# Two attention and expert layers on one core: the norm's small operations divided anew between GpSimd and VectorE, the output bias as a product of one row, and another order of the work

## The chip, the core and the metric

The kernel is one program on one core of a Trainium2 chip. Its engines are TensorE (PE; PEld is its weight load), VectorE (DVE), ScalarE (ACT), GpSimd (POOL) and SyncE (SP), which here only issues DMA transfers. The metric is the time of the whole program on the device in microseconds, lower is better; each version is run several times and the median counts.

## The reference, cut to what matters

Two transformer layers over x of 16 batches x 256 tokens x 128 channels, fp32, each with attention (16 heads of 8) and a mixture of experts, and a layer norm without scale or shift after every half:

```python
def _layernorm(x, axis=-1, eps=1e-05):
    m = jnp.mean(x, axis=axis, keepdims=True)
    v = jnp.var(x, axis=axis, keepdims=True)
    return (x - m) / jnp.sqrt(v + eps)
...
x = _layernorm(x + _L0_attn_ref(x, ...))   # causal, no bias
x = _layernorm(x + _L0_ffn_ref(x, ...))    # 8 experts, top 2, hidden 256, relu
x = _layernorm(x + _L1_attn_ref(x, ...))   # not causal; w_out, b_out
x = _layernorm(x + _L1_ffn_ref(x, ...))    # 15 experts, top 3, gated gelu, and a shared expert
```

The bias of the second attention's output, `out @ w_out.T + b_out`, is what the change calls the output bias (the value bias is folded into it: `bias_rows`, `bias_add`).

## The kernel before, in words

**Steps.** The program is a list of some 3,990 named steps, such as `qk(a)`, `scores(a, p)` or `gather(q, blk, k)`. `plan()` names each step's engine and predecessors; the table `BEGINS` gives each a time of beginning in hundredths of a microsecond, and `lay_out` sorts the steps by it. These times are keys of an order and nothing else. Every engine runs its own steps in that order and waits on semaphores inside each; a step that waits holds everything behind it on its engine, SyncE's and GpSimd's DMA issues too. Between the steps of TensorE stand `WARM` entries, bursts of 128x512 products of ones (L1537), 242 in all.

**Attention.** Batch a = 0 to 15 is the first layer, 16 to 31 the second. `qk` makes queries and keys; `qk_hi`, `qk_rest`, `qk_mid`, `qk_low` split them into three bf16 parts. `spread_parts(a)` (L994) sends them to memory and `stack(a)` (L1009, six transfers) brings them back as 48 rows for eight pairs of heads. `scores(a, p)` and `row_max(a, p)` (L1586) find each query's maximum, which `max_neg`, `max_T`, `max_keep` and `max_rows(a)` (L1016, two transfers) put beside the keys; then `scores_T(a, p)`, `exp(a, p)` (L1218), `weigh_V` (L1404), `O_T`, `O_norm`, `O_back`, `O_back_keep`, `proj` (L1430) and `sum` (L1619).

**Norm.** `stats(k, q)` on VectorE takes the statistics and their aggregate (L1632, L1635); `inverse_std(k, q)` on GpSimd adds epsilon (L1108), negates the mean (L1109), raises to -0.5 (L1111) and multiplies both (L1113); `normalise(k, q)` on ScalarE applies it (L1253). k = 0 is the norm after attention, k = 1 after the experts. The 16 last norms (k = 1, q from 16) differ: VectorE adds epsilon (L1638), GpSimd raises two batches at once (L1102), VectorE normalises (L1646).

**Experts.** `x_T2`, `logits`, `route_top`, `route_hot`, `ranks`, `route_rank`, `route_pos_mul`, `route_pos` place each token on pages of 256 rows; `route_diff`, `route_exp`, `route_weight` make its weight. `scatter` (L1149, GpSimd) writes tokens to the page buffer `xs`, which `clear_xs(k)` (L980, SyncE, 22 transfers of 512 KB) fills with zeros first. `table(i)` and `table_row(i)` (L1747, L1022) say which expert owns a page. `x_load`, `w_load` (L1038), `page_T`, `fc1` (L1486), `activate`, `fc2` (L1498), `page_keep`, `page_store` (L1056) work off 108 pages in three groups: batches 0 to 7, 8 to 15 and 16 to 31. `gather` (L1163, GpSimd) fetches a token's results and `combine` (L1791) adds them. `build_w1(k)` (L985 to L988, SyncE) copies the second layer's expert weights into one table in eight pieces of three transfers. `residual_bias(a)` (L1092) adds the output bias to x on GpSimd, once for each batch of the second layer.

Of the kernel before, what the change touches and what calls it, by code (L numbers as in the profile page):

```python
# [9 lines left out]
ALU = mybir.AluOpType  # L10
# [3 lines left out]
NB = 16  # L14
T = 256
D = 128
# [209 lines left out]
def plan():  # L226
# [10 lines left out]
    def norm(kind, q, t, after):  # L237
        last = kind == 1 and q >= NB
        add(t, "DVE", 0.8 if last else 0.71, 0.1, "stats", kind, q, after=after)
        if not last or power_batches(q):  # L240
            add(t + PRM["norm"][0], "POOL", 0.76 if last else 1.45, 0.1, "inverse_std", kind, q, after=[("stats", kind, q)])
        add(t + PRM["norm"][1], "DVE" if last else "ACT", 0.55 if last else 0.81, 0.1, "normalise", kind, q,
            after=[("inverse_std", kind, q + 1 if last and not power_batches(q) else q)])

    def attention(a, t):
# [10 lines left out]
        x = [("load_xT", a), ("load_consts",)] if L == 0 else [("x_T_keep", a), ("load_later",)]  # L256
# [35 lines left out]
        add(t + pj[2], "PE", 0.56, 0.25, "proj", a, after=[("O_back_keep", a), ("residual_bias", a)] + [("load_x", i) for i, (lo, hi) in enumerate(X_PIECES) if lo <= a < hi],  # L292
# [115 lines left out]
    for b in range(NB):  # L408
# [8 lines left out]
    "load_x": (3936, 5173, 7563, 10838,),  # L417
    "load_later": (5993,),
    "prepare": (7562,),
    "bias_rows": (10638,),  # L420
    "bias_add": (10690,),
    "build_w1": (9858, 10628, 12703, 15096, 16526, 17957, 19532, 21073,),
    "clear_xs": (5233, 5283, 5943, 6438, 7622, 7672, 10068, 10118, 10898, 10948, 12913, 12963, 15306, 15356, 16736, 16786, 18166, 18216, 19742,
        19792, 21556, 21606,),
    "load_xT": (0, 42, 1415, 2245, 3244, 6745, 8164, 9409, 10999, 13030, 14578, 16065, 17476, 19954, 21515, 25665,),
    "qk": (922, 2026, 3021, 4013, 5072, 7612, 8805, 9864, 12531, 14111, 15200, 16703, 18246, 20823, 22543, 26343, 28727, 30936, 32258, 33253, 36798,
        38253, 39534, 43076, 46491, 48104, 49075, 51012, 52231, 54201, 56839, 58521,),
    "qk_hi": (1140, 2244, 3243, 4135, 5194, 7734, 8927, 9982, 12649, 14233, 15333, 16825, 18368, 20945, 22665, 26461, 28850, 31054, 32376, 33371,
        36920, 38371, 39656, 43198, 46613, 48226, 49197, 51134, 52367, 54323, 56961, 58639,),
    "qk_rest": (1203, 2307, 3306, 4280, 5321, 8003, 8990, 10143, 12849, 14360, 15449, 17072, 18495, 21148, 22792, 26524, 28936, 31303, 32525, 33515,  # L430
        37337, 38553, 39845, 43285, 46755, 48386, 49357, 51276, 52521, 54593, 57200, 58815,),
    "qk_mid": (1276, 2380, 3379, 4353, 5394, 8076, 9072, 10217, 12954, 14433, 15522, 17145, 18568, 21267, 22905, 26642, 29027, 31506, 32678, 33606,
        37428, 38644, 39994, 43453, 46937, 48496, 49448, 51383, 52612, 54684, 57382, 58923,),
    "qk_low": (1342, 2446, 3454, 4427, 5485, 8223, 9138, 10290, 13078, 14575, 15617, 17240, 18659, 21375, 22971, 26708, 29102, 31674, 32744, 33793,
        37544, 38744, 40098, 43519, 47012, 48566, 49582, 51533, 53042, 54857, 57577, 59087,),
    "spread_parts": (1456, 2519, 3527, 4526, 5558, 8296, 9211, 10364, 13151, 14648, 15690, 17313, 18810, 21448, 23045, 26831, 29175, 31747, 32817,
# [1454 lines left out]
```

## Time and profile before

| | |
|---|---|
| median of 3 runs | 905.49 us (899.75 to 909.22) |
| profiled execution | 905.51 us, span of its instructions 903.7 us |
| busy: PE, DVE, ACT, POOL | 773.8, 652.9, 500.9, 426.0 us |
| granted TensorE clock, mean | 0.96 |
| DMA | 144.56 MB, mean 160 GB/s |
| chain of waits: PE, DVE, DMA, issue, POOL, ACT | 27, 11, 6, 6, 3, 3% of the span |

Busy time is a sum over the whole span, PE's with the warm-up products in it. The chain of waits follows back what released the last instruction. It names the engine that was late each time, not how much later the next one would have been. In a timeline row the bracket gives the engine's idle time before the instruction and who ended it.

### The profile page before, as it was taken

Reading aid. Unit: us, or ns where it says so; the run is one execution under the profiler, and the core shown is the slowest. Engines: PE = TensorE matmul, PEld = TensorE weight load, DVE = VectorE, ACT = ScalarE, POOL = GpSimd, SP = SyncE. Lnnn points to the kernel's source line nnn. Section 1 sums busy time; section 2 is a strip of 40 time slices with the busy share of each in tenths; the row PEclk is TensorE's granted clock in tenths of the full one; section 3 lists DMA queues with packets and bytes.
Section 4 is the critical chain, followed back from the end, with each engine's and each line's share of the span. In section 5 each row is a group of like instructions: output and inputs, shape, how many; then the busy total and the mean of one; then the engine's idle time right before and its main releaser. Section 6 shows DMA issues by size and latency. Waiting matters only on the chain.

```text
span 903.7 us, 23670 instructions
## 1 busy us (share of the span) xinstructions
PE 773.8 (86%) x7908; PEld 514.9 (57%) x7908; DVE 652.9 (72%) x1916; ACT 500.9 (55%) x971; POOL 426.0 (47%) x654
## 2 busy tenths in 40 slices
PE   3799999887999889998999999989888898999900
PEld 2456556545777555554775655544444587789800
DVE  1768777776666579898668899889884354688845
ACT  2157557444656557577666877776656344444300
POOL 4002341242203665576235673567567501677775
PEclk9999989999999999999999999999999999999955
DMA  5796774788777555637875664525241189996723
GB/s 121 131 260 137 191 208 125 202 200 209 197 185 187 126 119 120 154 87 190 212 202 146 174 139 96 112 51 124 55 120 42 48 249 291 329 290 181 213 64 111
DMA packets 118775, 144.56 MB, mean 160 GB/s; under 512 B 13155, under 2 KB 92673, under 8 KB 118657
## 3 DMA queue, kind: packets, MB, share of 16 engines
q1 hardware_dynamic: 108417, 122.06, 52.0%
q0 software_dynamic: 10240, 20.99, 8.7%
q8 instruction: 67, 1.10, 0.5%
q14 instruction: 51, 0.42, 0.2%
HBM read 89.78 MB, written 54.41 MB: 160 GB/s over the span
## 4 chain that ended last, share of the span: by engine, by line
PE 27%; DVE 11%; DMA 6%; issue 6%; POOL 3%; ACT 3%; SPq 0%; POOLq 0%; DVEq 0%; ACTq 0%
DMA G<-yd,ypos 4%; DVE mp L1586 4%; PE bank_N L1498 3%; PE bank_O L1404 3%; PE bank_FH L1486 3%; ACT P L1218 2%; PE pair_T L1385 2%; POOL xs L1149 2%; PE pair_S L1363 2%; PE pair_T L1486 2%; DVE X L1791 2%; PE bank_O L1486 1%; PE pair_S L1486 1%; PE pair_T L1498 1%; PE bank_M L1475 1%
## 5 line engine op out<-in xcount | busy, mean ns | idle before, releaser
L1586 DVE TENSOR_REDUCE mp<-pair_S 128x4 f32<-128x1024 f32 (+1 forms) x248 | 270.3, 1090 | 73.6 <-PE pair_S L1363 71.9
L1218 ACT ACTIVATE P<-pair_T 128x768 f32<-128x768 f32 (+1 forms) x256 | 234.4, 916 | 97.0 <-PE pair_T L1385 93.4
L1163 POOL DMA_INDIRECT G<-yd,ypos x160 | 154.0, 962 | 109.4 <-DMA yd<-yb 57.1
L1149 POOL DMA_INDIRECT xs<-X,ypos x160 | 159.0, 994 | 80.3 <-issue 44.1
L1404 PE MATMUL bank_O<-P,V 128*18 128x256 f32 (+1 forms) x2048 | 112.0, 360 | 1.4 <-ACT P L1218 1.4
L1385 PE MATMUL pair_T<-QK 51*128 51x256 bf16 (+1 forms) x1024 | 95.8, 262 | 11.0 <-ACT P L1218 8.9
L1363 PE MATMUL pair_S<-QK 48*128 48x256 bf16 (+1 forms) x992 | 92.9, 264 | 7.5 <-DVE mp L1586 5.9
L1108 POOL TENSOR_TENSOR rstd<-mv,half 128x2 f32<-128x2 f32 x48 | 9.5, 198 | 167.4 <-DVE mv L1635 167.2
L1404 PEld LDWEIGHTS bank_O<-P,V 128*18 128x18 f32 x2048 | 54.7, 99 | 43.9 <-issue 13.0
L1791 DVE SCALAR_TENSOR_TENSOR X<-G,wk,X 128x128 f32<-128x128 f32 x160 | 56.2, 352 | 31.6 <-DMA G<-yd,ypos 28.2
L1385 PEld LDWEIGHTS pair_T<-QK 51*128 51x128 bf16 x1024 | 47.0, 96 | 33.5 <-ACT P L1218 24.2
L1363 PEld LDWEIGHTS pair_S<-QK 48*128 48x128 bf16 x992 | 37.1, 96 | 40.4 <-DVE mp L1586 23.6
L1347 PE MATMUL pair_T<-bmat 64*128 64x128 bf16 (+1 forms) x544 | 47.7, 252 | 12.9 <-DMA QK<-mrow 7.3
L1498 PE MATMUL bank_N<-W,hT 128*128 128x128 f32 x368 | 52.7, 287 | 3.4 <-DVE X L1619 2.9
L1347 PE MATMUL pair_S<-bmat 64*128 64x256 bf16 x480 | 42.3, 254 | 15.3 <-DMA QK<-stk 9.6
L1537 PE MATMUL bank_M<-bmat 128*128 128x512 bf16 x193 | 54.6, 387 | 0.2 <-issue 0.2
L1225 ACT ACTIVATE OT<-bank_O 128x256 f32<-128x256 f32 x64 | 24.3, 380 | 51.3 <-PE bank_O L1404 51.1
L1486 PE MATMUL bank_FH<-xpT,W 128*128 128x256 f32 x184 | 50.8, 399 | 1.4 <-issue 1.2
L1498 PEld LDWEIGHTS bank_N<-W,hT 128*128 128x128 f32 x368 | 45.9, 194 | 10.8 <-issue 4.1
L1270 ACT ACTIVATE hT<-bank_FH,W 128x256 f32<-128x256 f32 x92 | 38.6, 471 | 20.5 <-PE bank_FH L1486 19.9
L1324 PE MATMUL bank_M<-xT,wqk 128*128 128x256 f32 x128 | 40.3, 441 | 7.3 <-DMA wqk<-wqk_in 4.2
L1253 ACT ACTIVATE X<-X,rstd 128x128 f32<-128x128 f32 x96 | 41.9, 487 | 6.6 <-POOL rstd L1113 6.2
(178 smaller groups left out, 1432.8 us busy)
## 6 DMA issues: line engine op xcount, KB each, us to landing
QK<-wtab SPq DMA_DIRECT2D x62, 257.0 KB, 3.8
W<-w_in SPq DMA_DIRECT2D x46, 321.0 KB, 3.9
yd<-yb SPq DMA_DIRECT2D x53, 256.0 KB
stk<-parts SPq DMA_DIRECT2D x32, 384.0 KB
QK<-stk SPq DMA_DIRECT2D x64, 192.0 KB
xs<-zeros SPq DMA_DIRECT2D x19, 512.0 KB, 7.4
xp<-xs SPq DMA_DIRECT2D x33, 256.0 KB, 5.2
QK<-stk SPq DMA_DIRECT2D x64, 128.0 KB
```

The lines of the kernel that those rows point to most:

```text
L1149: pool.indirect_dma_start(xs[g % 2][0:reach(a) * PAGE], bass.IndirectOffsetOnAxis(ypos[L][:, 2 * b + blk, k:k + 1], 0), X[:, 2 * b + blk, ...
L1163: pool.indirect_dma_start(G[i][:, blk, k, :], None, yd[g][0:reach(q) * PAGE], bass.IndirectOffsetOnAxis(ypos[L][:, 2 * b + blk, k:k + 1], 0))\
L1218: act.activation(P[:, i:i + 2, 0:n], pair["T"][:, :].rearrange("p (h c) -> p h c", h=2)[:, :, 0:n], ACT.Exp, scale=SCALE)\
L1347: pe.matmul(diagonal(banks[lane])[:, :, at:at + n], pick[i][rows, :], m[rows, :].unsqueeze(1).broadcast_to((HALF, 2, n)), start=(i == 0), ...
L1363: m = pe.matmul(banks[lane][:, o:o + n], QK[rows, a % NQK, 0, p, qb * D:(qb + 1) * D], QK[rows, a % NQK, 1, p, 0:n], start=(a >= NB), stop ...
L1385: m = pe.matmul(banks[lane][:, o:o + n], QK[rows, a % NQK, 1, p, kb * D:(kb + 1) * D], QK[rows, a % NQK, 0, p, T - n:T], start=(a >= NB), ...
L1404: m = pe.matmul(O[32 * j:32 * j + VW, q:T], w, x, start=(kb == 0 and lane == 0), stop=(kb == 1 and lane == 1), skip_group_check=True)
L1486: m = pe.matmul(H[:, c * T:(c + 1) * T], w_of(n)[:, c * D:(c + 1) * D], xpT[:, n % RT, :])
L1498: m = pe.matmul(Y[:, blk * D:(blk + 1) * D], hT[:, n % RH, c, blk * D:(blk + 1) * D], w[:, W_2[L] + c * D:W_2[L] + (c + 1) * D], start=(c ...
L1537: pe.matmul(B[:, :], ones, bmat[:, 0:4 * D], start=True, stop=True, skip_group_check=True)
L1586: dve.tensor_reduce(mp[:, a % 2, 0:n, :, 0, p].rearrange("p a r -> p r a"), S, AX.X, ALU.max, negate=True)\
L1791: dve.scalar_tensor_tensor(out=t, in0=G[i][:, blk, k, :], scalar=wk[L][:, b, blk, k:k + 1], in1=t, op0=ALU.mult, op1=ALU.add).then_inc(sig ...
```

## The change

There are four edits.

- **Norm.** For the 48 norms other than the last 16, VectorE now negates the mean and adds epsilon, behind a wait for its own aggregate; GpSimd raises to the power and multiplies.
- **Bias.** `residual_bias` is gone. `proj(a)` for a from 16 first multiplies a row of ones by the bias row into bank N, then accumulates its two products on it. The step `proj` now comes after `bias_add`. A memset makes the row of ones.
- **Order.** Every table of `BEGINS` is new. The least number of steps that leave their place is 233 of 1,346 on TensorE (its warm-up entries counted), 221 of 944 on VectorE, 200 of 856 on ScalarE, 94 of 441 on GpSimd and 137 of 387 on SyncE; most go one to four places.
- **Warm-up.** 240 products instead of 242, 93 entries in both. Between `x_T(16)` and `x_T(24)` there are 19 instead of 28.

```diff
-        add(t, "DVE", 0.8 if last else 0.71, 0.1, "stats", kind, q, after=after)
+        add(t, "DVE", 0.8 if last else 0.87, 0.1, "stats", kind, q, after=after)
...
-            add(t + 0.5, "POOL", 0.76, 0.1, "residual_bias", a, after=[("x_T", a), ("bias_add",)])
...
-    "table": (19781, 38113, 61772, 67284,),
-    "table_row": (19874, 38264, 61865, 67377,),
...
+    "table": (20242, 38279, 63895, 70637,),
+    "table_row": (20336, 38774, 65233, 70730,),
...
             def inverse_std(k, q):
                 r = rstd[:, k, q, :, :]
                 if last_norm(k, q):
                     n = power_batches(q)
-                    pool.wait_ge(var_ready.sem, var_ready.all(q - NB))
+                    pool.wait_ge(var_ready[k].sem, var_ready[k].all(q))
...
-                pool.wait_ge(aggregated[k].sem, aggregated[k].all(q))
-                pool.tensor_tensor(r[:, 0, :], mv[:, k, q, :, 1], half[:, 1, :], ALU.add).then_inc(powered[k].sem, 1)
-                pool.tensor_scalar(r[:, 2, :], mv[:, k, q, :, 0], -1.0, None, ALU.mult).then_inc(powered[k].sem, 1)
-                pool.wait_ge(powered[k].sem, powered[k].at(q, 1))
-                pool.tensor_tensor(r[:, 1, :], r[:, 0, :], half[:, 0, :], ALU.pow).then_inc(powered[k].sem, 1)
+                pool.wait_ge(var_ready[k].sem, var_ready[k].all(q))
+                pool.tensor_tensor(r[:, 1, :], r[:, 0, :], half[:, 0, :], ALU.pow).then_inc(powered[k].sem, 3)
                 pool.wait_ge(powered[k].sem, powered[k].at(q, 3))
+                pool.wait_ge(negated[k].sem, negated[k].all(q))
                 pool.tensor_tensor(r[:, 3, :], r[:, 2, :], r[:, 1, :], ALU.mult).then_inc(powered[k].sem, 1)
...
             def proj(a):
                 N = free("N")
                 pe.wait_ge(onT_kept.sem, onT_kept.all(a))
+                if a >= NB:
+                    pe.wait_ge(bv_ready.sem, 3)
+                    pe.matmul(N[:, 0:T], one_row[0:1, :], rows[0:1, R_BO:R_BO + D].unsqueeze(1).broadcast_to((1, 2, D)),
+                              start=True, stop=False, skip_group_check=True)
                 for blk in range(2):
                     m = pe.matmul(N[:, blk * D:(blk + 1) * D], OnT[:, blk * D:(blk + 1) * D],
-                                  wvo[:, a // NB, D:2 * D])
+                                  wvo[:, a // NB, D:2 * D], start=a < NB, stop=True, skip_group_check=a >= NB)
                 m.then_inc(proj_ps.sem, 1)
...
             def stats(k, q):
...
-                if last_norm(k, q):
-                    dve.wait_ge(aggregated[k].sem, aggregated[k].all(q))
-                    dve.tensor_scalar(rstd[:, k, q, 0, :], mv[:, k, q, :, 1], EPS, None, ALU.add).then_inc(var_ready.sem, 1)
+                dve.wait_ge(aggregated[k].sem, aggregated[k].all(q))
+                if not last_norm(k, q):
+                    dve.tensor_scalar(rstd[:, k, q, 2, :], mv[:, k, q, :, 0], -1.0, None, ALU.mult).then_inc(negated[k].sem, 1)
+                dve.tensor_scalar(rstd[:, k, q, 0, :], mv[:, k, q, :, 1], EPS, None, ALU.add).then_inc(var_ready[k].sem, 1)
```

The order at the places the text below comes back to, as the two tables give it:

```
SyncE    before  max_rows(7) build_w1(3) clear_xs(12) clear_xs(13) stack(9) spread_parts(10) load_xT(11)
                 build_w1(4) clear_xs(14) clear_xs(15) stack(10)
         after   max_rows(7) stack(9) spread_parts(10) clear_xs(12) load_xT(11) clear_xs(13) clear_xs(14)
                 build_w1(3) stack(10)
SyncE    before  stack(11) max_rows(9) spread_parts(12) build_w1(6) clear_xs(18) clear_xs(19) table_row(0)
                 load_xT(13) stack(12) max_rows(10)
         after   stack(11) max_rows(9) clear_xs(17) clear_xs(18) spread_parts(12) build_w1(5) build_w1(6)
                 load_xT(13) clear_xs(19) table_row(0) max_rows(10) stack(12)
VectorE  before  row_max(19,3) sum(16) combine(6,0) row_max(19,4) stats(0,16) route_pos(15) combine(6,1) table(1)
         after   row_max(19,3) table(1) combine(6,0) sum(16) row_max(19,4) stats(0,16) route_pos(15) combine(6,1)
SyncE    before  stack(20) table_row(1) w_load(23) w_load(24) w_load(25) w_load(26) spread_parts(21) max_rows(19)
         after   stack(20) table_row(1) spread_parts(21) max_rows(19) x_load(12) w_load(23) stack(21)
VectorE  before  route_hot(31) route_weight(31) route_rank(31) table(3) route_pos(31)
         after   route_hot(31) route_rank(31) route_pos(31)
GpSimd   before  ... gather(31,1,2), then inverse_std(1,17), (1,19), (1,21), ... (1,31)
         after   ... gather(28,1,0) inverse_std(1,17) ... gather(31,0,2) inverse_std(1,19) ... gather(31,1,2),
                 then inverse_std(1,21), ... (1,31)
VectorE  after   page_keep(103) normalise(1,16) activate(106) combine(28,0)
```

## Rows read from the trace of the kernel before

**Rows 1.** Busy us by stretch (length): PE, PEld, DVE, ACT, POOL; clock, DMA share, GB/s

```profile
67.00:310.00 243.00, 219.70 (x2873) 147.69 (x2867) 169.45 (x494) 141.91 (x273) 70.59 (x131) 0.96 0.71 179
310.00:500.00 190.00, 177.86 (x1838) 114.28 (x1840) 156.27 (x445) 132.26 (x266) 106.78 (x174) 1.00 0.60 151
500.00:670.00 170.00, 153.56 (x1581) 83.44 (x1577) 150.86 (x447) 120.04 (x210) 103.55 (x173) 0.98 0.49 114
...
720.00:860.00 140.00, 131.05 (x821) 115.63 (x819) 97.22 (x290) 58.51 (x144) 70.47 (x75) 1.00 0.82 254
```

**Rows 2.** Groups by line: the warm-up products

```profile
L1537 PE MATMUL bank_M<-bmat 128*128 128x512 bf16 x193 | 54.6, 387 | 0.2 <-issue 0.2
```

**Rows 3.** Instructions in order of time: GpSimd, then VectorE, in the tail

```profile
782.03 0.94 POOL L1163 DMA_INDIRECT G<-yd,ypos  x1 [2.31 <-DMA yd<-yb]
...
886.96 7.21 POOL L1102 TENSOR_TENSOR rstd<-rstd,half 128x4 f32<-128x4 f32 x7
...
892.97 5.23 DVE L1646 TENSOR_SCALAR X<-X,mv,rstd 128x128 f32<-128x128 f32 x20
```

**Rows 4.** In order of time: first and last of one norm's four on GpSimd

```profile
701.21 0.19 POOL L1108 TENSOR_TENSOR rstd<-mv,half 128x2 f32<-128x2 f32 x1 [0.33 <-DVE mv L1635]
...
702.38 0.20 POOL L1113 TENSOR_TENSOR rstd<-rstd 128x2 f32<-128x2 f32 x1
```

**Rows 5.** Groups by line: what GpSimd does per norm and per bias

```profile
L1111 POOL TENSOR_TENSOR rstd<-rstd,half 128x2 f32<-128x2 f32 x48 | 34.8, 724 | 0.0
...
L1092 POOL TENSOR_TENSOR X<-X,rows 128x256 f32<-128x256 f32 x16 | 11.6, 728 | 9.8 <-PE bank_M L1311 9.5
```

**Rows 6.** Line 1638 alone, ns min/median/max; and where it stands in time

```profile
L1638 DVE TENSOR_SCALAR rstd<-mv x16: 168/169/295, 781.9 to 892.9; 128x2 f32<-128x2 f32 x16
...
892.89 0.17 DVE L1638 TENSOR_SCALAR rstd<-mv 128x2 f32<-128x2 f32 x1
```

**Rows 7.** GpSimd's first norm operation by stretch: its busy us and count

```profile
67.00:310.00 243.00, 2.52 (x13) 0.96 0.71 179
310.00:500.00 190.00, 3.28 (x16) 1.00 0.60 151
500.00:670.00 170.00, 3.31 (x17) 0.98 0.49 114
670.00:720.00 50.00, 0.39 (x2) 1.00 0.12 41
```

**Rows 8.** Chain of waits: start us, us, what (four passes, two products)

```profile
727.36 0.87 PE bank_FH L1486 x4
```

**Rows 9.** In order of time: SyncE's queue and TensorE, first attention

```profile
155.05 4.71 SPq L980 DMA_DIRECT2D xs<-zeros  x2
159.87 4.89 SPq L1009 DMA_DIRECT2D QK<-stk  x6
...
170.93 0.34 PE L1347 MATMUL pair_S<-bmat 64*128 64x256 bf16 x4 [2.35 <-DMA QK<-stk]
...
212.88 1.54 SPq L1016 DMA_DIRECT2D QK<-mrow  x2
...
223.05 0.34 PE L1347 MATMUL pair_T<-bmat 64*128 64x128 bf16 x4 [2.61 <-DMA QK<-mrow]
```

**Rows 10.** In order of time: VectorE's table of pages, then SyncE's queue

```profile
401.86 1.22 DVE L1586 TENSOR_REDUCE mp<-pair_S 128x4 f32<-128x1024 f32 x1
...
406.43 0.28 DVE L1747 SCALAR_TENSOR_TENSOR owner<-ends,cols 128x64 f32<-128x64 f32 x1
...
414.04 3.72 SPq L1038 DMA_DIRECT2D W<-w_in  x4
417.86 0.39 SPq L994 DMA_DIRECT2D stk<-parts  x1
```

**Rows 11.** In order of time: GpSimd's last six scatters, first and last

```profile
712.06 1.00 POOL L1149 DMA_INDIRECT xs<-X,ypos  x1 [1.91 <-DVE ypos L1738]
...
718.43 0.96 POOL L1149 DMA_INDIRECT xs<-X,ypos  x1 [0.30 <-issue]
```

More of the change, by code:

```diff
@@ L238, in norm @@
         last = kind == 1 and q >= NB
-        add(t, "DVE", 0.8 if last else 0.71, 0.1, "stats", kind, q, after=after)
+        add(t, "DVE", 0.8 if last else 0.87, 0.1, "stats", kind, q, after=after)
         if not last or power_batches(q):
-            add(t + PRM["norm"][0], "POOL", 0.76 if last else 1.45, 0.1, "inverse_std", kind, q, after=[("stats", kind, q)])
+            add(t + PRM["norm"][0], "POOL", 0.76 if last else 1.0, 0.1, "inverse_std", kind, q, after=[("stats", kind, q)])
         add(t + PRM["norm"][1], "DVE" if last else "ACT", 0.55 if last else 0.81, 0.1, "normalise", kind, q,
@@ L291, in attention @@
         add(t + 0.3, "ACT", 0.33, 0.1, "O_back_keep", a, after=[("O_back", a)], frees="N")
-        add(t + pj[2], "PE", 0.56, 0.25, "proj", a, after=[("O_back_keep", a), ("residual_bias", a)] + [("load_x", i) for i, (lo, hi) in enumerate(X_PIECES) if lo <= a < hi],
+        add(t + pj[2], "PE", (0.56, 1.05)[L], 0.25, "proj", a, after=[("O_back_keep", a), ("bias_add",) if L else ()] + [("load_x", i) for i, (lo, hi) in enumerate(X_PIECES) if lo <= a < hi],
             bank="N")
@@ L426 @@
[L426 to L436, printed above, removed]
[3 rows of a table removed]
@@ new lines @@
+    "spread_parts": (1456, 2519, 3548, 4538, 5712, 8313, 9252, 10959, 13283, 14662, 15787, 17661, 19401, 21613, 23399, 27131, 29539, 32084, 33139,
[3 rows of a table added]
+    "v_keep": (1414, 1594, 1974, 6772, 8212, 9614, 11185, 13313, 14943, 16361, 17761, 20058, 21807, 25972, 28282, 30479, 31959, 33279, 35208, 38063,
+        39394, 42199, 44587, 47807, 49706, 50983, 53033, 54718, 56624, 58602, 60354, 62324,),
+    "stack": (1878, 2961, 3986, 4960, 6450, 8735, 9674, 12162, 13829, 15206, 16587, 18257, 20495, 22323, 23950, 27553, 29961, 32434, 33627, 34997,
+        38549, 39997, 42384, 45046, 48243, 49898, 51701, 53032, 55961, 57576, 59430, 61314,),
@@ new lines @@
+    "scores": (2883, 2960, 3236, 3312, 3546, 3643, 3723, 3810, 3946, 3985, 4139, 4288, 4322, 4461, 4611, 4696, 4995, 5326, 5391, 5498, 5715, 5959,
[12 rows of a table added]
+    "row_max": (2980, 3067, 3377, 3547, 3612, 3700, 3787, 3875, 4028, 4116, 4203, 4351, 4498, 4586, 4673, 4761, 5032, 5388, 5393, 5552, 5956, 5961,
[12 rows of a table added]
+    "max_neg": (3975, 4861, 6453, 8300, 10340, 11801, 13370, 14975, 17412, 18446, 20102, 21770, 23404, 25020, 27005, 30879, 33190, 35256, 37041,
+        39527, 41692, 44775, 46892, 49213, 51299, 53344, 55210, 57312, 59149, 60996, 63229, 65019,),
@@ L862, in build @@
         aggregated = [signal(f"aggregated{k}", 2) for k in range(2)]
-        var_ready = signal("var_ready")
+        var_ready = [signal(f"var_ready{k}") for k in range(2)]
         powered = [signal(f"powered{k}", 4) for k in range(2)]
+        negated = [signal(f"negated{k}") for k in range(2)]
         normed = [signal(f"normed{k}", 2) for k in range(2)]
@@ L938, in build @@
         LATE_LOADS = 3
-        FILLS = 3 + 3 * 2
+        FILLS = 4 + 3 * 2
         block = ctx.enter_context(nc.Block())
@@ L1615, in add_up @@
                     wait_x(dve, b)
-                else:
-                    dve.wait_ge(bias_added.sem, bias_added.all(b))
                 t = X[:, 2 * b:2 * b + 2, :]
```

230 lines of the change are left out of this document (113 added, 117 removed), and 244 rows, old and new, of tables (BEGINS, WARM).

## The prediction

> **What bounds the kernel now.** I read the table by stretch first, then the norm's own rows, then the waits at four places where the order is changed. The table [rows 1] says that no engine bounds the whole. Up to 310 us TensorE is busy nine tenths of the time, but part of that is filler: 193 warm-up products of 387 ns go to bank M alone [rows 2]. From 500 to 670 us VectorE is the fullest, 150.9 of 170 us, with TensorE at 153.6 including its filler. From 720 to 860 us TensorE runs the expert pages, 131 of 140 us; after them only GpSimd and VectorE compute. The reader should see three limits in series, so a gain in one stretch is worth nothing in another. After the last scatter the end is a chain: GpSimd issues gathers without a pause except where it waits for the pages of batch 18, at 782.03 us, and after the last gather at 886.96 us it raises nine variances to a power, while VectorE normalises back to back to 898.2 us [rows 3]. What comes before the last scatter therefore shifts the end almost one for one, and the tail itself only changes if VectorE has less to do there.
>
> **The change, part by part.** The sum is made against the profiled execution, 905.5 us with a span of 903.7; that is also the median of the runs.
>
> *GpSimd.* A norm takes it from 701.21 to 702.58 us, 1.37 us for four operations; the power (0.72 us) and the last product (0.20) stay, with the 80 ns between them, so 1.0 is left and 0.37 goes [rows 4, 5]. That is 48 norms x 0.37 = 17.8 us, and the bias goes with 16 x 0.73 = 11.6 us [rows 5]. Most of this buys nothing, since GpSimd is busy for only 106.8 of 190 and 103.6 of 170 us [rows 1]. It pays where scatters queue up behind one another, after about 640 us: two norms after 670 us and, at 17 in 170 us, three in the 30 us before [rows 7]. 5 x 0.37 = -1.9 us.
>
> *VectorE.* It adds two operations of two elements per norm. The last norms already have one of them: 169 ns median, starting right after the aggregate, and the next instruction starts 80 ns after it [rows 6]. The second costs 80 to 170 ns more, plus the wait on the aggregate. I take 0.28 us a norm; the ends are 0.16 (both at the 80 ns pitch) and 0.41 (both at full length with the wait), because the same form stands in the rows. 48 x 0.28 = 13.4 us busy. What of it is on the path goes by stretch, with the norms counted there [rows 7]: 17 norms in the stretch at 89% busy count in full, 4.8; 16 in the stretch at 82% by half, 2.2; 13 before it by a quarter, 0.9. Sum +7.9 us (4.5 to 11.6 by the two ends). The norm's latency hardly moves: 0.37 us leave GpSimd and about 0.3 come in on VectorE, so ScalarE's normalise and the scatters behind it start when they did.
>
> *TensorE.* The bias is now a product of one row over 256 columns in fp32, 16 times. Two such products take 0.87 us in a page [rows 8], so one is 0.43 if one row costs what 128 do; the ends are 0.39, what a bf16 product of 512 columns takes [rows 2], and 0.87, if a single one took as long as the pair. 16 x 0.43 = 6.9 us (6.2 to 13.9). It stands behind the wait for the transposed O, so it delays that batch's sum; a third of TensorE's extra time reaching the end is my choice, between none (filler stands next to it) and all of it: +2.3. The stretch of batches 16 to 23 gets 9 warm-up products fewer, 3.5 us [rows 2], by the same third -1.2.
>
> The parts alone: -1.9 + 7.9 + 2.3 - 1.2 = **+7 us**.
>
> *Order, first attention.* SyncE's queue is where it hurts. Before stack(9), its six copies, stand a table piece and two fills of the scatter buffer: the two fills hold the queue from 155.05 for 4.71 us and the stack leaves only at 159.87; its scores are the ones TensorE waits for: 2.35 us, until 170.93 [rows 9]. After the change stack(9) and spread_parts(10) stand ahead of all of them, earlier by the fills' 4.71 and the piece, and that wait is gone. max_rows(10) left at 212.88, behind the six copies of stack(12); TensorE waited 2.61 us for it at 223.05 [rows 9]. It now goes ahead of them, but one more table piece stands ahead of both, so I take 1.5 of the 2.61. Sum -3.9 us. Against it: three fills and a piece now stand ahead of stack(10), where two fills and a piece stood; a fill costs the queue 2.4 us here [rows 9], so this can hand a wait of the same size to batch 10.
>
> *Order, second attention.* table(1) stands behind a sum, two combines, a row maximum and a statistic and runs at 406.43; SyncE then waits for its row, issues four weight loads in 3.72 us, and spread_parts(21) leaves only at 417.86 [rows 10]. Now table(1) follows row_max(19,3) directly, which ends at 403.08, so 3.35 us earlier, and spread_parts(21) stands ahead of the weight loads, which saves their 3.72 us as well. Late next is stack(22), which is moved past seven more issues. TensorE has only filler and small gaps to win there. I take -3 us (0 to -7).
>
> *Order, end of routing.* Batch 31's weights and table(3) stood between its one-hot and its positions; both go behind. GpSimd's idle 1.91 us before the last six scatters goes, less one small operation moved in: -1.6 us [rows 11].
>
> *Order, tail.* The powers of the pairs 17 and 19 go between gathers. Each delays the gathers by its 1.03 us and is missing later, and VectorE's four early normalises free 2.1 us of its back-to-back run, which the later start eats: 0. What covers it: the early normalise of batch 16 now waits for GpSimd's 76th gather ahead of activate(106), so the last two pages finish some 10 us later, still before the gathers of batch 31, the last six, read them. If that cover is gone, the gathers wait for a page's store, as they do for 2.31 us at 782.03 [rows 3].
>
> *The other moves.* Of VectorE's 944 steps 221 leave their place in the order, of ScalarE's 856 200, of SyncE's 387 137, most by one to four places. From the stretches' idle time on TensorE, 12.1 us at 310 to 500 and 16.4 at 500 to 670 [rows 1], a sixth may be recovered, 4.8 us; it may be lost just as well. I take -5, with ends -18 and +10.
>
> **Sum:** 905.5 + 7 - 3.9 - 3 - 1.6 - 5 = **899 us**.
>
> **The rivals.** *The order does more (chance 0.30).* The stalls after each freed wait close as well: ScalarE and VectorE stand idle where TensorE waits, and the other moves give 14 us instead of 5. For it: gaps on TensorE in every stretch. Against: VectorE's 89%. 899 - 10 = **889 us**.
>
> *The gains are absorbed (0.20).* Freed waits in the first attention only let batches run into the next fill on SyncE, table(1) only uncovers the next wait, and of the named moves just the end of routing counts, with the other moves' 5: 905.5 + 7 - 1.6 - 5 = **906 us**.
>
> *VectorE becomes the bound (0.14), slower.* Place: 500 to 670 us and the stretch before. If row maxima, pages and norms share a full VectorE, all 35 norms from 310 us on and the 16 bias products are paid in full, 35 x 0.41 + 16 x 0.43 = 21 us, and stack(10) and stack(22) are held by their new neighbours for 4 us more; with -3 for the table and -1.6 for the routing, 905.5 + 20.4 = **926 us**. It decides from the point where VectorE has no idle slice left between row maxima; now it has 19 us in 170 [rows 1].
>
> *The port rule (0.02).* A two-element VectorE operation of the last norms took 168 ns at least, 169 in the median and 295 at most over 16, while GpSimd was issuing gathers the whole time [rows 6]; nothing waits for GpSimd there. Were each of the 96 new operations held for half of a scatter issue of 0.96 us [rows 11], 46 us would be added, of which by the shares above (7.9 of 13.4) 27 reach the end: 899 + 27 = 926 us. The Trainium skill, SBUF — State Buffer, section "SBUF: two separate sides", says that VectorE in a two-port mode and GpSimd exclude each other for a whole instruction. By that rule the small operations would queue behind scatters; the trace shows one of 16 that might have.
>
> *The change doesn't do what it says (0.01):* the order is a table of times, and if the program sorted it as before, only the parts would act: 905.5 + 7 = 912 us.
>
> **How the numbers follow.** My forecast, 899, has 0.33. Its own range, 890 to 908, is the sum with the VectorE ends (-3, +4) and the order's ends partly cancelling. Over all cases 881 to 917 leaves out about 2 in 10. One per cent, about 9 us (what a measurement of this kernel can tell from no change), puts the borders at 896.4 and 914.6. Faster by more: most of 889 and a third of the forecast, 0.39. Slower by more: the two slow cases and a little of the others, 0.17. Between: 0.44.
>
> **What would show it.** Norm rows: two GpSimd operations of 0.72 and 0.2 us, VectorE's total up by 11 to 15 us, GpSimd's down by 28 to 30. Before stack(9) no fill, and no wait of TensorE near 170 us; if a wait of 2 us or more stands before batch 10's scores, the gain moved on. The last scatter issue, now at 718.43, should start near 712, and the time from it to the end should stay within 2 us of today's 185. In the stretch at 500 to 670 us, VectorE above 95% busy speaks for the slower rival. I am wrong if the last scatter comes after 720, or if the pages, not the routing, move the end.

## The result, and the profile after

The changed kernel takes 931.39 us (median of 4, 928.76 to 943.39) against 904.21 for the kernel before in the same set, a ratio of 1.029 (95% interval 1.022 to 1.036): 27 us slower, where 899 was forecast. Its profiled execution took 932.4 us with a span of 930.6. A time in us is the median of all runs of a kernel, while a ratio leaves out the slow ones, more than 1.5% above the fastest of their kernel, so the two need not agree exactly.

The table by stretch, its borders after 670 us moved with the work (columns as in [rows 1]):

```profile
67.00:310.00 243.00, 210.38 (x2725) 145.27 (x2737) 166.28 (x508) 132.98 (x258) 60.84 (x101) 0.92 0.68 174
310.00:500.00 190.00, 169.54 (x1701) 112.45 (x1709) 146.31 (x434) 124.31 (x252) 89.58 (x123) 0.96 0.63 153
500.00:670.00 170.00, 153.87 (x1567) 87.60 (x1582) 152.68 (x471) 119.92 (x218) 87.21 (x127) 0.97 0.45 103
...
745.00:890.00 145.00, 136.68 (x829) 119.54 (x829) 96.18 (x283) 58.24 (x147) 75.35 (x80) 0.99 0.81 248
```

Against [rows 1] TensorE is busy 9 us less up to 310 us and 8 us less up to 500, and the granted clock is lower in both stretches (0.92 for 0.96, 0.96 for 1.00). VectorE is no fuller than forecast, 152.7 of 170 us. So the time is not in an engine that is full; TensorE stands still more often. These are its waits of more than 1.9 us between 100 and 750 us, from its instructions in order of time (start us, us; in the bracket the wait and who ended it):

```profile
109.41 0.50 PE L1338 MATMUL pair_T<-bmat 64*128 64x128 bf16 x4 [3.35 <-DMA QK<-mrow]
...
151.44 0.50 PE L1338 MATMUL pair_S<-bmat 64*128 64x256 bf16 x4 [3.77 <-DMA QK<-stk]
...
187.62 0.50 PE L1338 MATMUL pair_T<-bmat 64*128 64x128 bf16 x4 [3.50 <-DMA QK<-mrow]
...
220.47 1.94 PE L1315 MATMUL bank_M<-xT,wqk 128*128 128x256 f32 x4 [3.51 <-DMA xT<-xT_in]
...
230.91 0.51 PE L1338 MATMUL pair_S<-bmat 64*128 64x256 bf16 x4 [1.94 <-DMA QK<-stk]
...
303.23 0.66 PE L1413 MATMUL bank_N<-cols,On 128*128 128x128 f32 x2 [3.52 <-DVE On L1602]
...
332.28 1.12 PE L1481 MATMUL bank_FH<-xpT,W 128*128 128x256 f32 x4 [2.43 <-issue]
...
437.57 0.66 PE L1470 MATMUL bank_M<-cols,xp 128*128 128x128 f32 x2 [3.68 <-DMA xp<-xs]
...
496.96 1.94 PE L1481 MATMUL bank_FH<-xpT,W 128*128 128x256 f32 x4 [3.41 <-issue]
...
546.90 0.39 PE L1376 MATMUL pair_T<-QK 51*128 51x256 bf16 x4 [3.63 <-DMA QK<-mrow]
...
729.88 1.01 PE L1446 MATMUL bank_N<-cols,xG 128*128 128x15 f32 x4 [3.19 <-ACT xG L1231]
```

Eleven waits, 35.9 us in all, nine of them over 3 us, six of these nine for a transfer of SyncE's queue. In the same stretch the kernel before had five over 1.9 us, 11.8 us in all, and none over 2.7; two of them stand in [rows 9]. The steps that wait are scores_T(4,0), scores(8,0), scores_T(8,0), qk(13), scores(12,0), O_back(11), an fc1, page_T(25), fc1(38), scores_T(23,0) and logits(31). The "issue" before an fc1 names no releaser; that step waits for its weights or the transposed page.

Behind such a wait TensorE runs slower. Around the wait of 437.57 us, in slices of 5 us (the last three figures are granted clock, DMA share, GB/s):

```profile
430.00:435.00 5.00, 3.84 (x37) 2.12 (x29) 4.12 (x14) 4.25 (x10) 2.94 (x5) 1.00 1.05 139
435.00:440.00 5.00, 2.43 (x13) 1.60 (x14) 0.33 (x1) 1.53 (x3) 1.91 (x2) 0.56 0.98 325
440.00:445.00 5.00, 5.00 (x21) 3.60 (x21) 3.34 (x10) 1.72 (x5) 0.39 (x2) 0.50 0.05 20
445.00:450.00 5.00, 5.00 (x40) 4.01 (x39) 3.63 (x13) 2.71 (x7) 0.00 (x0) 0.91 0.24 48
```

From 440 to 445 us TensorE is busy throughout and gets 21 matmuls through where the next slice has 40: the clock is 0.50, its lower level of 1.2 GHz. What the clock withholds is worked out from such slices of 5 us as 5 times (1 - granted clock), for those below 0.97 up to 860 us: 15 us in the kernel before, 39 in the changed one. These slices hold time in which TensorE waits as well; counted over its busy time alone, the same sum is 13 and 31 us. The waits and the withheld clock therefore overlap and are not to be added up.

When each batch's exponentials begin (read from ScalarE's instructions in order of time) shows where the delay arises:

| batch | before | changed | changed - before | parts_again | sync_again | fill_waits |
|---|---|---|---|---|---|---|
| 6 | 144.6 | 141.6 | -3.0 | 144.1 | 146.7 | 139.1 |
| 13 | 303.8 | 310.0 | +6.2 | 301.9 | 304.3 | 297.5 |
| 19 | 425.0 | 429.1 | +4.1 | 423.4 | 427.0 | 418.7 |
| 20 | 457.2 | 469.1 | +11.9 | 458.2 | 467.8 | 454.6 |
| 23 | 526.4 | 547.3 | +21.0 | 528.3 | 548.5 | 539.5 |
| 31 | 679.3 | 701.3 | +22.0 | 684.9 | 707.1 | 691.2 |

The last scatter comes at 744.40 us instead of 718.43; from it to the end of the span it is 186.2 us instead of 185.3.

### The profile page after: what moved, and what is told of

It is laid out like the page before. It is cut to its first block, busy times and chain, and to the rows that moved or that the text cites. A ratio compares the mean times of both kernels' runs of the same rounds, so it can differ in the third digit from the quotient of the medians.

```text
span 930.6 us, 23729 instructions
## 1 busy us (share of the span) xinstructions
PE 785.8 (84%) x7887; PEld 532.7 (57%) x7938; DVE 662.4 (71%) x2012; ACT 497.7 (53%) x973; POOL 399.4 (43%) x543
## 4 chain that ended last, share of the span: by engine, by line
PE 50%; DVE 15%; SPq 11%; DMA 10%; issue 8%; ACT 4%; POOL 1%; DVEq 0%; POOLq 0%; ACTq 0%
PE bank_O L1395 7%; DVE mp L1581 6%; PE bank_FH L1481 5%; PE bank_N L1493 5%; PE pair_T L1376 4%; PE pair_S L1354 4%; SPq L1008 3%; DMA QK<-stk 3%; PE bank_M L1532 3%; ACT P L1209 3%; PE bank_M L1315 2%; DMA G<-yd,ypos 2%; SPq L1015 2%; PE pair_T L1338 2%; PE pair_S L1338 2%
## 5 line engine op out<-in xcount | busy, mean ns | idle before, releaser
L1101 POOL TENSOR_TENSOR rstd<-rstd,half 128x2 f32<-128x2 f32 x48 | 35.1, 732 | 195.0 <-DVE rstd L1632 194.4
L1395 PE MATMUL bank_O<-P,V 128*18 128x256 f32 (+1 forms) x2048 | 115.2, 368 | 1.4 <-ACT P L1209 1.4
L1376 PE MATMUL pair_T<-QK 51*128 51x256 bf16 (+1 forms) x1024 | 96.6, 265 | 13.9 <-ACT P L1209 8.9
L1338 PE MATMUL pair_T<-bmat 64*128 64x128 bf16 (+1 forms) x544 | 48.6, 257 | 13.9 <-DMA QK<-mrow 6.9
L1481 PE MATMUL bank_FH<-xpT,W 128*128 128x256 f32 x184 | 52.8, 412 | 7.1 <-issue 7.0
L1244 ACT ACTIVATE X<-X,rstd 128x128 f32<-128x128 f32 x96 | 42.0, 489 | 13.9 <-POOL rstd L1104 13.6
L1532 PE MATMUL bank_M<-bmat 128*128 128x512 bf16 x158 | 46.2, 405 | 3.2 <-issue 2.6
L1251 ACT ACTIVATE xpT<-bank_M 128x256 f32<-128x256 f32 x77 | 29.4, 382 | 36.2 <-PE bank_M L1470 35.8
```

What stands on the lines that cost most here:

```text
L1338: pe.matmul(diagonal(banks[lane])[:, :, at:at + n], pick[i][rows, :], m[rows, :].unsqueeze(1).broadcast_to((HALF, 2, n)), start=(i == 0), ...
L1376: m = pe.matmul(banks[lane][:, o:o + n], QK[rows, a % NQK, 1, p, kb * D:(kb + 1) * D], QK[rows, a % NQK, 0, p, T - n:T], start=(a >= NB), ...
L1395: m = pe.matmul(O[32 * j:32 * j + VW, q:T], w, x, start=(kb == 0 and lane == 0), stop=(kb == 1 and lane == 1), skip_group_check=True)
L1481: m = pe.matmul(H[:, c * T:(c + 1) * T], w_of(n)[:, c * D:(c + 1) * D], xpT[:, n % RT, :])
L1532: pe.matmul(B[:, :], ones, bmat[:, 0:4 * D], start=True, stop=True, skip_group_check=True)
```

## The experiments

**Two kinds of chips.** The kernels were run in sets, each with the kernel before beside them. The first set and the third ran on chips where the kernel before itself takes 1085 and 1087 us instead of 905. Engines there also stand still together, and the profile names only "remote" (another core or an unknown queue) or "issue" (nothing that it shows) for it. In order_only, for instance, ScalarE, VectorE and TensorE all stood until 406 us (12.21, 9.70 and 6.87 us):

```profile
406.21 0.38 ACT L1071 ACTIVATE xG<-bank_N 128x256 f32<-128x256 f32 x1 [12.21 <-remote]
406.27 1.23 DVE L1417 TENSOR_REDUCE mp<-pair_S 128x4 f32<-128x1024 f32 x1 [9.70 <-remote]
...
406.64 2.08 PE L1329 MATMUL bank_N<-W,hT 128*128 128x128 f32 x8 [6.87 <-ACT xG L1071]
```

What causes that was not tried. The eight kernels of these two sets are listed together and bear on the result at 905 us only as far as later runs repeat them.

*parts_only* is the changed kernel's code in the old order: the two tables are the only edit.

```diff
-BEGINS = {... the changed kernel's ...}    WARM = (... the changed kernel's ...)
+BEGINS = {... the kernel before's, without "residual_bias" ...}    WARM = (... the kernel before's ...)
```

> The changed kernel's code (norm with two operations on GpSimd and two on VectorE, bias as a product of one row), with every step and every warm-up burst in the order of the kernel before. Theory A, the order costs the time: the parts alone cost little, 904 to 912 us, and none of the six waits of 3 us or more that TensorE has after the 4th batch of the changed kernel appears. Rival B, the parts cost it (VectorE too full, the product in TensorE's way): 920 to 931 us. Rival C, only the two together cost it: 904 us, with order_only at 904 as well.

*order_only* is the reverse: the code of the kernel before with the changed kernel's tables and its own 16 `residual_bias` steps.

> The code of the kernel before (norm in four GpSimd operations, bias added by GpSimd) in the order and with the warm-up bursts of the changed kernel; the 16 bias steps stand where the kernel before has them against x_T. Theory A: 922 to 931 us, with the waits for stack, max_rows, xT and xp in TensorE's rows as in the changed kernel. Rival B: 904 to 910 us. Rival C: 904 us.

*order_first* and *order_second* cut the order at batch 13; the third set repeated them as *first_again* and *second_again*.

```diff
 # F = the steps that the kernel before begins ahead of exp(13,0)
+order_first:  F in the new order, then all others in the old
+order_second: F in the old order, then all others in the new
```

> The changed kernel's code; the steps that the kernel before begins up to the 14th batch's exponentials (about 304 us) in the new order, all later ones in the old. Theory A, with the loss read from the two traces: the exponentials of batch 13 were 6 us late and the 15 or so that follow come later, so 908 to 914 us. If a loss in the first half is made good later: 904 us. If the late part only suffers because the first half is late: 925 us or more.

> The changed kernel's code; the old order up to the 14th batch's exponentials, the new order behind. Theory A: 918 to 926 us, with TensorE's wait of some 3.7 us for the loaded page rows near 430 us still there and nearly all of the delay arising between the exponentials of batches 18 and 23. If the late part only suffers because the first half is late: 904 to 908 us.

*sync_only* gives SyncE alone the new order:

```diff
 # parts_only's tables, but
+SyncE: ... max_rows(7) stack(9) spread_parts(10) clear_xs(12) ... table_row(1) spread_parts(21) max_rows(19) x_load(12) ...
```

> The changed kernel's code; only SyncE's 387 steps stand in the new order, all other engines and the warm-up bursts in the old one. parts_again (nothing in the new order) was 914.7 us, both (everything) 933.3. Theory S, the queue of transfers carries the loss: 925 to 933 us, with waits of 3 us or more for stack, max_rows and xp. Rival, the order of TensorE's own steps and its warm-up bursts carries it: 912 to 918 us.

*pages_early* is the first of the two moves shown further down under two_moves.

> The same kernel as order_first: all engines in the new order up to the exponentials of batch 13, in the old one behind. From the traces at 905 us (changed kernel against parts_again) the new order was 8 us late there: 919 to 924 us. If what is lost there is given back: 915.

> The same kernel as order_second: the old order up to there, the new one behind. The traces have 11 us more delay in the second part (8 of them between the exponentials of batches 19 and 23): 924 to 928 us. If the second part was only late because the first was: 915.

> The changed kernel with one move on SyncE: x_load(13) and x_load(14) stand right behind x_load(12), ahead of two weight loads and stack(21), about as in the old order. Theory S: TensorE's wait of 3.7 us for xp at 437.6 us and the half clock of the 8 us behind it go, the exponentials of batch 20 come 5 to 7 us earlier, and 3 to 6 us of it reach the end: 927 to 930 us. Rival, TensorE only waits for the next thing instead: 932 to 934 us.

Measured, against 1085.4 us in the first set and 1087.2 in the third:

| kernel | us | ratio | 95% interval |
|---|---|---|---|
| parts_only | 1109.5 | 1.023 | 1.016 to 1.029 |
| order_only | 1085.4 | 0.998 | 0.995 to 1.002 |
| order_first, first_again | 1103.3, 1099.1 | 1.017, 1.010 | 1.006 to 1.027, 1.005 to 1.014 |
| order_second, second_again | 1109.6, 1101.7 | 1.023, 1.013 | 1.016 to 1.030, 1.005 to 1.022 |
| sync_only | 1108.4 | 1.008 | 1.001 to 1.014 |
| pages_early | 1093.4 | 1.010 | 1.006 to 1.015 |

The expectations were written for a kernel before of 905 us, so only the ratios can be held against them, and by these the cause is turned around: on these chips the edits cost 2.3% and the order nothing, as rival B had it, and sync_only is near its rival. That set by itself would have given the wrong cause for the result at 905 us; pages_early decides nothing. So the two halves were run again with the changed kernel beside them.

> [...]

> The same kernel as order_only, once more. Theory A: 1.02 to 1.03 of the kernel before where that takes 904 us. If the parts cost the time: 1.00.

> The changed kernel itself beside the two. 1.029 of the kernel before where that takes 904 us; where it takes 1085 us, 1.02 to 1.03 if the parts carry the loss there.

The kernel before took 906.15 us here. parts_again: 914.7, ratio 1.011 (1.008 to 1.015). order_again: 940.8, 1.039 (1.035 to 1.043). both: 933.3, 1.034 (1.027 to 1.041). So the edits cost 8.5 us in the old order and save 7.5 in the new one, and the new order costs 18.6 us with the edits and 34.7 without. (The saving is the least certain of these: the intervals of order_again and both overlap, and one of the four runs of both took 944.7 us.) The order carries the loss, theory A as to its place; its size for order_only was 10 us too small.

**norm_only** splits the edits: the code and order of the kernel before with the norm's hunks of the diff.

```diff
+                dve.wait_ge(aggregated[k].sem, aggregated[k].all(q))
+                if not last_norm(k, q):
+                    dve.tensor_scalar(rstd[:, k, q, 2, :], mv[:, k, q, :, 0], -1.0, None, ALU.mult).then_inc(negated[k].sem, 1)
+                dve.tensor_scalar(rstd[:, k, q, 0, :], mv[:, k, q, :, 1], EPS, None, ALU.add).then_inc(var_ready[k].sem, 1)
```

> The kernel before, in its own order, with the norm's edit alone (epsilon and negated mean by VectorE, two operations left on GpSimd); the bias is still added by GpSimd. By the forecast's terms -1.9 + 7.9: 910 to 912 us, and the bias product adds the other 1 to 3 of the 8.5 us of parts_again. Rival, the norm is free and the product carries it: 904 to 906 us.

911.8 us against 908.0 in this set, ratio 1.007 (1.003 to 1.011): 6.6 us by the ratio (3 to 10), 3.8 by the medians. That agrees with the forecast's term for the norm, and the product would be left with about 2 of parts_again's 8.5; the two ratios' intervals overlap, so the rest is no more than an indication.

**sync_again** and **fill_waits** ask by what path the order costs time. fill_waits is the changed kernel with ten more entries in `WARM`, so that TensorE is busy in its waits:

```diff
 WARM = (...
+ # ahead of scores_T(4,0), scores(8,0), scores_T(8,0), qk(13), O_back(11), page_T(25), fc1(38), scores_T(23,0)
+ (..., "M", 12) x8,
+ # ahead of scores(12,0)                  # ahead of logits(31)
+ (..., "M", 6),                           (..., "M", 10),
```

> The changed kernel with ten more bursts of warm-up products (112 products, some 0.22 us each at full clock, so 2.6 us a burst of 12), one straight ahead of each step at which TensorE waited 1.9 to 3.8 us in the changed kernel: scores_T(4,0), scores(8,0), scores_T(8,0), qk(13), scores(12,0), O_back(11), page_T(25), fc1(38), scores_T(23,0), logits(31). No wait is shortened; only TensorE is busy in it. Theory C, half of what a wait costs is the half clock of the 5 to 8 us behind it: those stretches keep the full clock and the time falls by 8 to 20 us, to 913 to 925 us. Rival, the waits alone are the cost: 931 to 935 us, or later by what the products overrun.

> The same kernel as sync_only (only SyncE's steps in the new order). Where the kernel before takes 905 us: theory S, the queue of transfers carries the loss, 925 to 933 us; rival, TensorE's own order and its bursts carry it, 912 to 918 us.

Against 903.5 us: fill_waits 918.5, ratio 1.017 (1.011 to 1.023), and sync_again 928.6, 1.026 (1.018 to 1.033). Both theories hold. Products that compute nothing give back about 11 to 15 of the 27 us. (The changed kernel was not in this set; the two ends are its ratios of 1.029 and 1.034 against 1.017.) SyncE's order alone carries about 13 of the 18.6 us: 1.026 against parts_again's 1.011, from another set. This is TensorE in fill_waits around page_T(25), the same step that waited 3.68 us in the changed kernel:

```profile
423.32 2.75 PE L1363 MATMUL bank_M<-bmat 128*128 128x512 bf16 x12
426.75 0.41 PE L1301 MATMUL bank_M<-cols,xp 128*128 128x128 f32 x2 [0.69 <-DMA xp<-xs]
...
427.86 1.13 PE L1312 MATMUL bank_FH<-xpT,W 128*128 128x256 f32 x4
```

The pages land no earlier against the work ahead of them, but the next fc1's four matmuls take 1.13 us, where the same four took 2.08 in the changed kernel (at 439.56), and the withheld clock falls from 39 to 10 us. In the table of batches fill_waits is 3 to 15 us ahead of the changed kernel. The Trainium skill says as much, TensorE: Matmul & The Clock Gate, section "HAM oscillation — how this bites in real kernels": waits for data let the clock fall, and the time at half clock comes on top of the wait. The traces agree here (0.50 behind the wait of 3.68 us, 1.00 with the wait filled).

sync_again shows the source of the waits. Most of its delay against parts_again arises at two places, 6.0 us between the batches 19 and 20 and 8.4 between 22 and 23 (its profiled run, 934.1 us, is the slowest of its four, and parts_again's, 911.2, the fastest). SyncE's instructions there in order of time (start us, us), in sync_again:

```profile
414.80 0.38 SPq L824 DMA_DIRECT2D stk<-parts  x1
419.18 1.49 SPq L846 DMA_DIRECT2D QK<-mrow  x2
420.77 0.39 SPq L880 DMA_DIRECT2D xp<-xs  x1
422.18 0.36 SPq L868 DMA_DIRECT2D W<-w_in  x1
422.64 2.22 SPq L839 DMA_DIRECT2D QK<-stk  x6
425.94 0.38 SPq L868 DMA_DIRECT2D W<-w_in  x1
426.36 0.46 SPq L880 DMA_DIRECT2D xp<-xs  x1
...
532.90 2.90 SPq L839 DMA_DIRECT2D QK<-stk  x6
535.84 1.55 SPq L846 DMA_DIRECT2D QK<-mrow  x2
```

and in parts_again, which has the old order:

```profile
412.04 3.81 SPq L868 DMA_DIRECT2D W<-w_in  x4
415.95 0.39 SPq L824 DMA_DIRECT2D stk<-parts  x1
416.40 1.68 SPq L846 DMA_DIRECT2D QK<-mrow  x2
418.18 1.40 SPq L880 DMA_DIRECT2D xp<-xs  x3
...
520.37 1.59 SPq L846 DMA_DIRECT2D QK<-mrow  x2
522.07 2.24 SPq L839 DMA_DIRECT2D QK<-stk  x6
```

In the old order three page loads go out together by 419.6 us; in the new one x_load(13) leaves at 426.36, behind two weight loads and a stack. And max_rows(23) went ahead of stack(25), now it goes behind its six copies; TensorE waited 6.52 us for it at 544.03.

**two_moves** puts these back and nothing else.

```diff
-SyncE: ... x_load(12) w_load(23) stack(21) w_load(24) x_load(13) w_load(25) x_load(14) x_load(15) w_load(26)
+SyncE: ... x_load(12) x_load(13) x_load(14) w_load(23) stack(21) w_load(24) w_load(25) x_load(15) w_load(26)
-SyncE: ... w_load(44) stack(25) max_rows(23)
+SyncE: ... w_load(44) max_rows(23) stack(25)
```

> The changed kernel with two moves on SyncE and nothing else: x_load(13) and x_load(14) stand right behind x_load(12), as in the old order, and max_rows(23) stands ahead of stack(25) instead of behind its six copies, as in the old order. In sync_again the exponentials fell back 8.6 us where TensorE waited 3.0 us for x_load(13)'s pages and 8.5 us where it waited 6.5 us for max_rows(23). Theory S: both waits go, and with the clock behind them 7 to 14 of the 931 to 933 us: 918 to 925 us. Rival, the next late transfer takes their place: 929 to 933 us.

928.5 us, ratio 1.026 (1.021 to 1.031), single runs from 922.1 to 930.9. Both waits are gone from the trace of the run of 922.1 us, and batch 23 comes 14.1 us late instead of 21.0. But the median lies between the theory's range and the rival's: against 1.029 and 1.034 for the changed kernel the gain is 3 to 8 us, and the intervals overlap. The places are shown in the trace, their worth in time is not settled.

**before_fills** does to the kernel before what fill_waits did:

```diff
 WARM = (...
+ # ahead of scores_T(0,0) 6, scores_T(4,0) 4, scores(9,0) 9, scores_T(10,0) 10, fc2(12) 10, max_T(15) 8, max_T(27) 8
```

> The kernel before with seven more bursts of warm-up products (55 products) ahead of the steps at which TensorE waited 1.2 to 2.6 us there: scores_T(0,0), scores_T(4,0), scores(9,0), scores_T(10,0), fc2(12), max_T(15), max_T(27). Theory C, the clock behind a wait costs time by itself: 2 to 6 us less than the kernel before, 0.993 to 0.998. Rival: the same or slower, since the waits are short and the products overrun them.

906.0 us against 903.5, ratio 1.001 (0.997 to 1.005): the rival. The withheld clock is 17 us there, not less than the 15 before: the clock fell at other, unfilled places instead, as at 215 to 225 us (0.52 and 0.50). No wait of TensorE between 100 and 750 us is longer than 1.9 us in its trace, and still nothing is won. Filling paid in the changed kernel, where nine of the ten waits took 3.2 to 3.8 us, and not for these of 1.2 to 2.6.

**first_fast** is order_first again, where the kernel before takes 908.

> The same kernel as order_first, where the kernel before takes 905 us: all engines in the new order up to the exponentials of batch 13, in the old one behind. Only SyncE in the new order cost 2.5 us up to there, all engines 8.2 us (against parts_again). If TensorE's own order carries the rest: 919 to 924 us, with a wait of 2 us or more for O_norm(11), behind which the new order puts O_back(11) with two steps between O_T and it.

926.4 us, ratio 1.020 (1.013 to 1.028). With 1.011 for the edits, the new order of the first attention alone costs 0.9%, 8 us, about as expected, though the two intervals overlap. The exponentials of batch 13 say the same: the changed kernel's are 8.1 us behind parts_again's. (In first_fast they are 15 us behind, 316.9 to 301.9, but its profiled run is the slowest of its four.) The waits for transfers are those of the changed kernel. One wait that the expectation put to the order is not the order's: O_back(11) stands behind O_T(11), v(14) and a weigh_V in both orders, and it waits 2.99 us for VectorE here, 3.52 in the changed kernel, but 3.04 in parts_again too, in the old order:

```profile
296.69 0.41 PE L1244 MATMUL bank_N<-cols,On 128*128 128x128 f32 x2 [3.04 <-DVE On L1433]
```

With the norm's edit alone that wait is 1.05 us (norm_only), in the kernel before 0.89. The second part of the order was not run by itself at 905 us, nor the order of TensorE's own steps.

**moves_and_fills** joins two_moves and seven of the ten bursts.

> The changed kernel with the two moves of two_moves and seven of the ten bursts of fill_waits (not those at the three steps of the stretch at 430 to 550 us, where the moves take two of the waits away). If wait and clock are the cost: 905 to 915 us, below fill_waits' 918.5 and two_moves' 928.5. If the fills and the moves save the same time: 917 to 920 us.

926.2 us, ratio 1.021 (1.014 to 1.029): neither. With the page loads ahead, something else is late:

```profile
435.68 2.04 PE L1312 MATMUL bank_FH<-xpT,W 128*128 128x256 f32 x4 [4.70 <-issue]
```

The pages' step does not wait any more; the next fc1 waits 4.70 us, and the clock falls to 0.50 again; this stretch had no burst in this kernel. The bracket names no releaser. Its weights are the likely one, since w_load(24) now leaves behind three page loads and a stack, but that is not shown. Here, at least, the moves only chose which step waits.

## Why the prediction was wrong

By its own steps, with what the runs showed:

- **GpSimd and VectorE, the norm.** Forecast +6.0 us (-1.9 and +7.9), measured 6.6 (norm_only, 3 to 10). The operations are there as forecast: on GpSimd 732 and 195 ns, on VectorE 183 and 177 ns.

```profile
L1101 POOL TENSOR_TENSOR rstd<-rstd,half 128x2 f32<-128x2 f32 x48 | 35.1, 732 | 195.0 <-DVE rstd L1632 194.4
...
L1632 DVE TENSOR_SCALAR rstd<-mv 128x2 f32<-128x2 f32 x64 | 11.3, 177 | 0.6
L1104 POOL TENSOR_TENSOR rstd<-rstd 128x2 f32<-128x2 f32 x48 | 9.3, 195 | 3.8
L1631 DVE TENSOR_SCALAR rstd<-mv 128x2 f32<-128x2 f32 x48 | 8.8, 183 | 1.7
```

  VectorE's busy time rose by 9.5 us (662.4 for 652.9) where 11 to 15 were named (11.4 in parts_again, 664.3), GpSimd's fell by 26.6 where 28 to 30 were. VectorE's total rises by less than the two groups' sum, since two such instructions overlap. The port rule doesn't carry the cost, though the trace tests it less often than the rival assumed: only 29 of the 112 additions and negations run while GpSimd issues a scatter or gather. The 83 others take 0.17 us at most; of the 29, ten take 0.20 to 0.42, about 1.5 us more in all, against half of a scatter issue (480 ns) on each of 96 that the rival took.

- **TensorE, the bias.** Mis-sized, of little weight. The product runs as two passes:

```profile
L1422 PE MATMUL bank_N<-rows,one_row 1*128 1x256 f32 x32 | 11.0, 423 | 0.3 <-ACT OnT L1222 0.2
```

  That is 11.0 us busy for 16, 0.69 each, where 0.43 was taken, half of what two products take in a page (6.9 in all), and 13.9 was the upper end. The parts together, without the warm-up's -1.2, which parts_again doesn't have, were forecast at +8.3 and measured at +8.5.

- **Order, first attention: -3.9 forecast, +8 measured (first_fast).** This is the first step that failed. Two waits were read off the old trace and credited as gains, and the wait near 170 us is indeed gone: stack(9) leaves at 152.16 instead of 159.87. But clear_xs(10) and build_w1(2), which stood ahead of spread_parts(8), now stand between it and stack(8); three fills and a piece stand between spread_parts(10) and stack(10), and another piece ahead of max_rows(8). Of the changed kernel, SyncE in order of time (start us, us):

```profile
139.14 8.55 SPq L1008 DMA_DIRECT2D QK<-stk  x6
...
169.55 6.75 SPq L1008 DMA_DIRECT2D QK<-stk  x6
...
178.73 6.16 SPq L1015 DMA_DIRECT2D QK<-mrow  x2
```

  Of the kernel before, two fills and then stack(8):

```profile
126.80 6.60 SPq L980 DMA_DIRECT2D xs<-zeros  x2
...
139.92 2.55 SPq L1009 DMA_DIRECT2D QK<-stk  x6
```

  The old order lets SyncE stand in the fills, before batch 8's parts are sent. Both stacks begin at 139 us, but in the new order the six copies hold SyncE for 8.55 us and the last leaves at 147.7 instead of 142.5; TensorE waits 3.77 us for them, and 3.50 us for max_rows(8), whose two copies took 6.16 us. The prediction named three fills and a piece ahead of stack(10) as a wait that might be handed on, with 2.4 us a fill, and put it into no term of its forecast. TensorE's own order seems to do the rest: it asks for scores(8,0) ahead of scores_T(6,4) and weigh_V(6,0) now, and with SyncE alone in the new order the copies take 6.39 us, and the wait is only 1.00 us (sync_again at 156.09).

- **Order, second attention: -3 forecast, +5 to +6 measured** (batches 19 to 20 against parts_again: 5.2 us in the changed kernel, 6.0 in sync_again). table(1) moved as said. For spread_parts(21), which left at 417.86, 7 us were credited, but the prediction did not ask when its own data is ready. VectorE makes the last part of it, in the kernel before and in the changed one:

```profile
412.70 0.68 DVE L1578 TENSOR_TENSOR parts<-rest,parts 128x512 bf16<-128x512 f32 x1
...
417.85 0.69 DVE L1573 TENSOR_TENSOR parts<-rest,parts 128x512 bf16<-128x512 f32 x1
```

  So the queue held it for 4.5 us, not 7. In the new order the queue is free and it leaves as soon as the data is there, at 414.80 us in sync_again and at 418.57 in the changed kernel, where the data is 5 us later. What the move did change is what now leaves late behind it, the page loads. "TensorE has only filler and small gaps to win there" was right, and no price was put on what it could lose.

- **Order, end of routing: -1.6 forecast, about +3 measured.** GpSimd's idle 1.91 us ahead of the last scatters is 0.45 now. But from batch 31's first exponential to the last scatter it takes 43.1 us (701.3 to 744.4), against 39.1 before and 39.9 in parts_again, with TensorE's 3.19 us for the copied xG at logits(31) in between. It takes 39.9 in sync_again too, so SyncE's order isn't what does it. That wait stands in the trace; that it is the cause was not isolated.

- **Order, tail: 0 forecast, +0.9 measured.** From the last scatter to the end 186.2 us instead of 185.3, within the 2 us named.

- **The other moves: -5 with ends -18 and +10.** The step that failed most. Over five hundred moves were taken as a share of TensorE's idle time that may be recovered, "lost just as well", and the likeliest value was set on the side of a gain with nothing in the profile for it. With the named moves and the warm-up, the order was forecast at -14.7 us. Measured, the whole of it costs 18.6 us with the edits and 34.7 without.

**What the sum left out** is the clock. Waits of TensorE were priced at their length, and the granted clock stood in the table of stretches without a term. The changed kernel has 24 us more of waits over 1.9 us and 24 us more of withheld clock; fill_waits, in which no wait is shortened, gives back about 11 to 15 of the 27 us. With such a term (24 us of clock beside 24 us of waits), the order's upper end of +10 would have stood at up to twice that; this is an estimate, since the two overlap. The slow rival had the right side and the wrong mechanism: VectorE is 152.7 of 170 us busy (90%), below the 95% named for it.

The sign that the text gave for being wrong, the last scatter after 720 us, is the one that came.

## What to carry to other kernels

Where an order written out by hand is changed, don't credit a wait that the trace shows before asking two things of the step that is moved: was its own data ready when the queue reached it, and which step of the waiting engine is asked for earlier by the new order. And price a wait of TensorE like those of 3 to 4 us here with the half clock behind it as well: while an order is being mended, a burst of products that compute nothing gives that part back (11 to 15 of 27 us here). Where the waits took 1.2 to 2.6 us it gave nothing (before_fills).

What one half of a change costs can depend on the other half (the edits cost 8.5 us in the old order and seem to save 7.5 in the new), and on the chip: run both halves and the whole on the same one.

## What the runs showed that was not expected

- The kernel before took 904 to 908 us in five sets and 1085 and 1087 in two, there with engines standing still together for up to 12 us. The edits cost 1.1% on the first kind and 2.3% on the second, the order 3.9% and nothing.
- What a transfer costs its queue is no constant. The six copies of a stack took SyncE 2.17 us in parts_again (at 139.20), 2.55 in the kernel before and 8.55 in the changed one, all for batch 8; the two copies of a max_rows took from 1.49 to 6.16 us. The fill issued ahead of the 8.55 us took 1.28 us itself, the two in the kernel before 6.60: the step that stands longest in the queue need not be the one that filled it. This is inferred from the order; the transfers in flight were not counted.
- Behind a wait of 3.68 us the clock was 0.50 for at least 5 us though TensorE was busy all the time; with 12 products of 0.22 us each in the wait it stayed at 1.00.
